# A convolution, a state space layer and a recurrence on one core: decay rates computed behind the first chunk, one zero fill a slot, one staging load for four blocks, a last step in halves

## What is computed

```
# layer 0, added to x: a causal "convolution" over time of cond, per feature, then a state space scan
conv  = conv_b + sum_k x_pad[:, k:k+L, :] * cond[k]        # K = 128 taps
proj  = conv @ Wp + bp ;  B_t = softplus(proj[:64]) ; C_t = tanh(proj[64:])
u     = x @ Ws + bs
A, dt = -softplus(A_log), softplus(dt_log) ; decay = 1 + dt * A      # 64 rates each
state = decay * state + dt * B_t * u_t ;  y_t = C_t * state
x     = x + y @ Wo + bo
# layer 1, added to x: a recurrence over time
h     = tanh(h @ Wh + x_t @ Wx + b)                        # 128 steps, h0 = cond
x     = x + hs
```

## Time and profile before

| | |
|---|---|
| three runs | 1167.56, 1169.76, 1170.22 us; median 1169.76 |
| profiled execution, its own time | 1169.48 us |
| its span in the trace | 1167.7 us |
| mean granted TensorE clock | 0.997 |
| PE busy | 1155.2 us |
| DVE, ACT, POOL busy | 698.9, 579.2, 355.5 us |

### The profile page before, as it was taken

How to read it: one execution, slowest core, us unless ns; L and a number is a source line. 1 busy time by engine, 2 the same in 40 slices (tenths; PEclk the granted TensorE clock), 3 DMA queues, 4 the chain that set the end, 5 groups by cost and what they waited for, 6 DMA issues and landing times.

```text
span 1167.7 us, 16204 instructions
## 1 busy us (share of the span) xinstructions
PE 1155.2 (99%) x6000; PEld 965.6 (83%) x6000; DVE 698.9 (60%) x1110; ACT 579.2 (50%) x856; POOL 355.5 (30%) x202
## 2 busy tenths in 40 slices
PE   8999999999999999999999999999999999999997
PEld 8998999976888888888888888888888888888886
DVE  7767776676555555556565555555555556565553
ACT  6755665574435454544454545435454544454431
POOL 5300005023233333333333333333333333333330
PEclk9999999999999999999999999999999999999999
DMA  8897777612022222222222222222222222222202
GB/s 304 288 328 263 255 262 240 204 35 82 6 97 83 99 77 72 72 72 72 72 72 72 72 72 72 75 97 83 98 77 72 72 72 72 72 72 72 73 36 72
DMA packets 71794, 130.12 MB, mean 111 GB/s; under 512 B 3728, under 2 KB 29328, under 8 KB 71760
## 3 DMA queue, kind: packets, MB, share of 16 engines
q1 hardware_dynamic: 71760, 129.65, 33.4%
HBM read 96.08 MB, written 33.55 MB: 111 GB/s over the span
## 4 chain that ended last, share of the span: by engine, by line
PE 96%; DVE 2%; ACT 1%; DMA 0%; issue 0%; POOL 0%; POOLq 0%; SPq 0%; DVEq 0%
PE bank L904 10%; PE bank L912 10%; PE bank L913 10%; PE bank L898 10%; PE bank L916 10%; PE bank L897 10%; PE bank L813 10%; PE bank L952 5%; PE bank L830 5%; PE bank L873 3%; PE bank L879 3%; PE bank L887 2%; PE bank L888 2%; PE bank L848 2%; PE bank L845 2%; PE bank L846 2%
## 5 line engine op out<-in xcount | busy, mean ns | idle before, releaser
L440 POOL TENSOR_TENSOR x_lo<-x_f,x_hi 128x512 fp32r<-128x512 f32 x128 | 161.8, 1297 | 588.2 <-ACT x_hi L537 588.2
L564 ACT ACTIVATE h_f<-z_f 128x512 f32<-128x512 f32 x128 | 80.9, 632 | 296.7 <-DVE z_f L751 296.7
L912 PE MATMUL bank<-wh_hi,hT_hi 128*128 128x512 f32 x512 | 200.7, 392 | 0.0
L760 DVE TENSOR_TENSOR hT_lo<-bank,hT_hi 128x512 fp32r<-128x512 f32 x128 | 88.5, 691 | 186.8 <-ACT hT_hi L568 186.8
L913 PE MATMUL bank<-wh_lo,hT_hi 128*128 128x512 f32 x512 | 200.0, 391 | 0.0
L898 PE MATMUL bank<-wx_lo,x_hi 128*128 128x512 f32 x512 | 199.7, 390 | 0.0
L897 PE MATMUL bank<-wx_hi,x_hi 128*128 128x512 f32 x512 | 199.6, 390 | 0.0
L751 DVE TENSOR_TENSOR z_f<-bank,b_rows 128x512 f32<-128x512 f32 x128 | 88.5, 691 | 132.3 <-PE bank L916 129.3
L434 POOL TENSOR_TENSOR x_lo<-x_f,x_hi 128x2048 fp32r<-128x2048 f32 x32 | 147.9, 4621 | 1.4 <-PE bank L813 1.4
L904 PE MATMUL bank<-wx_hi,x_lo 128*128 128x512 f32 x512 | 144.8, 404 | 0.3 <-POOL x_lo L440 0.3
L916 PE MATMUL bank<-wh_hi,hT_lo 128*128 128x512 f32 x512 | 137.0, 389 | 0.0
(11 more groups left out here) (93 smaller groups left out, 1682.7 us busy)
## 6 DMA issues: line engine op xcount, KB each, us to landing
x_f<-x_dtb SPq DMA_DIRECT2D x32, 1024.0 KB, 7.9
out<-x_f SPq DMA_DIRECT2D x31, 1024.0 KB, 5.3
ring<-x_rev SPq DMA_DIRECT2D x55, 512.0 KB, 5.2
ring<-hankel SPq DMA_DIRECT2D x44, 512.0 KB, 4.1
x_early<-x_rev SPq DMA_DIRECT2D x8, 512.0 KB, 7.1
t_low<-low_rows SPq DMA_DIRECT2D x4, 512.0 KB, 4.7
wx_f<-Wx SPq DMA_DIRECT2D x1, 1024.0 KB, 8.0
wh_f<-Wh SPq DMA_DIRECT2D x1, 1024.0 KB, 7.8
```

What stands on the lines that cost most here:

```text
L440: nc.gpsimd.tensor_tensor(x1_lo[:, c], x1_f[par][:, c], f(x1_hi[:, c]), ALU.subtract)\
L564: nc.scalar.activation(h_f[:], z_f[:], ACT.Tanh).then_inc(h_ready, 1)
L760: nc.vector.tensor_tensor(hT_lo[:], turned_h, f(hT_hi[:]), ALU.subtract).then_inc(htlo_ready, 1)
L912: nc.tensor.matmul(z, hT_hi[:, k], wh_hi[:, k], start=False, stop=False)
```

## The change

- One load of 512 KB stages the low rows of the first four blocks; it is issued first. The next ones are issued after the `x` of blocks 3, 7, 11 and 15, instead of before the `x` of blocks 2, 6, 10 and 14. `vec` is loaded after block 7's `x` and the third room's low rows, and before the first piece of `Wp`.
- One zero fill a slot, 96 partitions x 768 elements; all four slots before the first shift on DVE.
- The wait for `vec` and the rate instructions move behind chunk 0's copies; ACT's two run after its loop over chunk 1's copies, DVE's last three at the end of chunk 1's projections, ahead of the scaling of `Wo`.
- The last step runs in two halves of 256 columns: bias add, tanh, two transposes, residual add and store, each a half at a time, the two halves' transposes in different banks. `hT_hi` and `hT_lo` of the last step are not computed.

```diff
@@ sync, load_ring
-                if n < 4:
-                    sp.dma_start(low_room(0)[quarter(n)], low_rows[quarter(n)]).then_inc(first_low[n], DMA)
-                if n % 4 == 2 and n // 4 + 1 < SHIFTED // 4:
-                    ...
+                if n == 0:
+                    sp.dma_start(low_room(0), low_rows[0:P]).then_inc(lows_loaded[0], DMA)
                 if n >= SHIFTED:
                     sp.dma_start(t_rows, toeplitz(n)).then_inc(t_loaded[slot], DMA)
                 for half in (range(2) if n == 0 else range(1)):
                     ...
+                if n % 4 == 3 and n // 4 + 1 < SHIFTED // 4:
+                    ...
             for n in range(WIDE):
                 load_ring(n, n % RING)
-                if n == 1:
-                    sp.dma_start(vec[:], vectors).then_inc(vec_loaded, DMA)
+            sp.dma_start(vec[:], vectors).then_inc(vec_loaded, DMA)
@@ sync, last step
+                if last:
+                    rows = out[:, TIME - 1, :].rearrange("(c p) b -> p c b", p=P)
+                    for h in range(2):
+                        sp.wait_ge(out_ready, TIME + h)
+                        sp.dma_start(rows[:, 2 * h:2 * h + 2], x1_f[par][:, 2 * h:2 * h + 2, G - 1]).then_inc(stored[par], DMA)
@@ scalar: the rates
             shift(0)
             shift(1)
-            act.wait_ge(rate_step, 1)
-            ...
-            act.wait_ge(vec_loaded, DMA)
             for m in range(0, BANKS, 2):
                 ...
+            act.wait_ge(vec_loaded, DMA)
             for m in range(BANKS):
                 copy_conv(1, m)
                 copy_turned(0, m)
                 ...
+            act.wait_ge(rate_step, 1)
+            nc.scalar.activation(rates_e[:], rates[:, 0:2], ACT.Exp).then_inc(rate_act, 1)
+            act.wait_ge(rate_act, 1)
+            nc.scalar.activation(rates[:, 2:4], rates_e[:], ACT.Ln, bias=1.0).then_inc(rate_act, 1)
@@ scalar: the last step
+                    if last and s == G - 1:
+                        for h in range(2):
+                            act.wait_ge(zsum_ready, t + 1 + h)
+                            nc.scalar.activation(h_f[:, half_of(h)], z_f[:, half_of(h)], ACT.Tanh).then_inc(h_ready, 1)
+                        continue
@@ vector
             def zero(slot):
-                nc.vector.memset(t_part(slot)[quarter(0), :, 0:3 * Q], 0.0)
-                nc.vector.memset(t_part(slot)[quarter(1), :, 0:2 * Q], 0.0)
-                nc.vector.memset(t_part(slot)[quarter(2), :, 0:Q], 0.0).then_inc(t_zeroed, 1)
+                nc.vector.memset(t_part(slot)[0:3 * Q, :, 0:3 * Q], 0.0).then_inc(t_zeroed, 1)
 ...
-            zero(0)
+            for slot in range(RING):
+                zero(slot)
             shift(0)
-            zero(1)
             shift(1)
-            zero(2)
-            zero(3)
-            dve.wait_ge(vec_loaded, DMA)
-            ...
@@ vector: the last step
+                    if last and s == G - 1:
+                        for h in range(2):
+                            nc.vector.tensor_tensor(z_f[:, half_of(h)], ZB[s % 2][:, half_of(h)], b_rows[:, half_of(h)], ALU.add)\
+                              .then_inc(zsum_ready, 1)
+                        for h in range(2):
+                            dve.wait_ge(ht_done, t + 1 + h)
+                            end = x1_f[par][:, 2 * h:2 * h + 2, s, :]
+                            nc.vector.tensor_tensor(end, last_turned(h).rearrange("p (c b) -> p c b", c=2), end, ALU.add)\
+                              .then_inc(out_ready, 1)
+                        continue
@@ tensor: the last step
+                    if end:
+                        for h in range(2):
+                            pe.wait_ge(h_ready, t + 1 + h)
+                            for k in range(2 * h, 2 * h + 2):
+                                mm = nc.tensor.transpose(HB[1 - h][:, bass.ts(k, P)], h_f[:, bass.ts(k, P)], ident[:])
+                            mm.then_inc(ht_done, 1)
+                        continue
```

More of the change, by code:

```diff
@@ L192, in conv_at, with half_of, last_turned @@
             return conv[:, :, t] if c == 2 else conv[:, t]
+        def half_of(h):
+            return slice(h * D // 2, (h + 1) * D // 2)
+        def last_turned(h):
+            return HB[1 - h][:, half_of(h)]
         def turn_bank(c, m):
@@ L301, in load_ring @@
                 t_rows = ring[:, slot, 0].rearrange("p (j k) -> p j k", j=CH // 2)
-                if n < 4:
-                    sp.dma_start(low_room(0)[quarter(n)], low_rows[quarter(n)]).then_inc(first_low[n], DMA)
-                if n % 4 == 2 and n // 4 + 1 < SHIFTED // 4:
+                if n == 0:
+                    sp.dma_start(low_room(0), low_rows[0:P]).then_inc(lows_loaded[0], DMA)
+                if n >= SHIFTED:
+                    sp.dma_start(t_rows, toeplitz(n)).then_inc(t_loaded[slot], DMA)
+                for half in (range(2) if n == 0 else range(1)):
+                    some = CH // 2 if n == 0 else CH
+                    sp.dma_start(x_part(n)[:, half * some:(half + 1) * some], x_rev[:, bass.ds(n * CH + half * some, some), :])\
+                      .then_inc(x_part_loaded[x_slot(n)] if half == 0 else second_half, DMA)
+                if n % 4 == 3 and n // 4 + 1 < SHIFTED // 4:
                     k = n // 4 + 1
@@ L355, in stores_and_loads @@
                     load_x(g + 2, par)
-                for s in range(0, G, 1 if last else G):
+                for s in range(0, G - 1 if last else G, 1 if last else G):
                     n = 1 if last else G
@@ L381, in shift @@
                     pool.wait_ge(wp_ready, 2)
-                pool.wait_ge(first_low[n] if n < 4 else lows_loaded[n // 4], DMA)
+                pool.wait_ge(lows_loaded[n // 4], DMA)
                 if n >= RING:
@@ L463, in shift @@
                     act.wait_ge(t_zeroed, n + 1)
-                act.wait_ge(first_low[n] if n < 4 else lows_loaded[n // 4], DMA)
+                act.wait_ge(lows_loaded[n // 4], DMA)
                 if n >= RING:
@@ L597, in shift @@
                     dve.wait_ge(t_zeroed, n + 1)
-                dve.wait_ge(first_low[n] if n < 4 else lows_loaded[n // 4], DMA)
+                dve.wait_ge(lows_loaded[n // 4], DMA)
                 if n >= RING:
@@ L646, in _ @@
                 copy_conv(0, m)
+            dve.wait_ge(vec_loaded, DMA)
+            nc.vector.scalar_tensor_tensor(out=rates[:, 0:2], in0=logs, scalar=-1.0, in1=logs, op0=ALU.mult, op1=ALU.min)\
+              .then_inc(rate_step, 1)
             for c in range(KC - 1):
@@ L655, in _ @@
                 if c == 1:
+                    dve.wait_ge(rate_act, 2)
+                    nc.vector.scalar_tensor_tensor(out=rates_e[:], in0=logs, scalar=0.0, in1=rates[:, 2:4], op0=ALU.max, op1=ALU.add)\
+                      .then_inc(rate_step, 1)
+                    dve.wait_ge(rate_step, 2)
+                    nc.vector.tensor_tensor(rates[:, 0:1], rates_e[:, 0:1], rates_e[:, 1:2], ALU.mult).then_inc(rate_step, 1)
+                    dve.wait_ge(rate_step, 3)
+                    nc.vector.tensor_scalar(rates[:, 1:2], rates[:, 0:1], -1.0, 1.0, ALU.mult, ALU.add).then_inc(rate_step, 1)
                     dve.wait_ge(ws_wo_loaded, 2 * DMA)
```

17 lines of the change are left out of this document (1 added, 16 removed).

## The result

The changed kernel takes 1162.91 us (median of 6, 1162.57 to 1163.3) against 1169.97 for the kernel before (6 runs, 1167.56 to 1171.29). (In runs 4 and 8 of the experiments and in the kernel before beside runs 1 to 4, one execution each took over 3000 us; the ratios leave it out, and it moves the medians by 0.12 at most.) The ratio is 0.9941, 95% interval 0.9928 to 0.9954: 6.9 us faster, between 5.4 and 8.4. The forecast was 5.1 us and 1164.4; the time lies 0.3 us inside the lower end of the wide range (1162.6) and under the lower end of the forecast's own (1163.2). The profiled execution took 1162.89 us against 1169.48, 6.6 less, and those are what the two traces share out.

What follows compares the result with a forecast made beforehand. PE, busy 99% of the span, was taken as the bound, with some 12 us winnable at the ends. 1169.48 - 3.15 (start) - 1.95 (end) = 1164.4 us; own range 1163.2 to 1165.4, wide range 1162.6 to 1167.0.

Steps and rivals of the forecast that it cites:

- the pause ahead of block 2: Start: PE idle from 10.63 to 13.54 us behind ACT's late bank copy; the clock's fall loses 1.6 us more.
- The start: Up to block 16: it starts at 37.35 instead of 40.50, held by DMA landings, winning 3.15 us (bounds 0.55 to 4.0).
- the landing rule: First DMAs: a load lands when as many KB were asked for before and with it, whatever they are.
- rival B: Behind block 4: DMA engines take the front's gain back, leaving 1.45 us; time 1166.1, or 1167.0 at 318 GB/s; chance 0.15.
- the new wait ahead of block 4: Low rows land at 13.65, ACT's shift and copy take 1.65, so PE starts block 4 at 15.35 instead of 18.75.
- Block 0: Start: the staging load lands at 4.4, so PE starts block 0 at about 6.4, 1.3 us later than before.
- The rates' new place: Chunks 1 and 2: late rate instructions cost nothing, ACT being idle and DVE having 0.85 us of cover for 0.54.
- The end: Last step: halves and dropping `hT_hi` and `hT_lo` win 1.95 us, bounds 1.3 and 2.4.
- S: Slower: low rows of blocks 4 to 7 land after 19.2; with block 4 at 22, 1172 us; chance 0.03.
- C: Start: PE's idle time ahead of block 0 delays the clock one stretch, costing about 1 us; 1165.5; chance 0.10.
- D: End: halves don't do what they say, winning 1.0 to 1.3 instead of 1.95; 1165.2; chance 0.07.
- F: Faster still: landings 0.9 us sooner without vec's 13-element rows, and a last landing of 1.6; 1163; chance 0.05.

Runs made afterwards that it cites:

- run 4: Changed kernel with three zero fills a slot instead of one, all four slots still ahead of DVE's first shift; 1166.87 us, ratio 0.9978.
- run 8: Kernel before with only the single staging load and the new order of the low rows; 1170.35 us, ratio 1.0003.
- run 1: Changed kernel with the last step whole again, as before the change; 1164.51 us, ratio 0.9958.
- run 2: Changed kernel with the rates computed ahead of chunk 0 again and vec loaded after block 1's x; 1163.17 us, ratio 0.9947.
- run 3: Changed kernel with the low rows in four 128 KB quarter loads and the old load order again; 1165.53 us, ratio 0.9974.
- run 9: Kernel before with only the rates and vec moved behind chunk 0; 1167.93 us, ratio 0.9987.
- run 10: Changed kernel plus an unneeded 256 KB load to partitions 0 to 63, behind block 1's x; 1164.45 us, ratio 0.9961.
- run 11: Changed kernel plus an unneeded 256 KB load to partitions 32 to 95, behind block 1's x; 1162.64 us (two executions), ratio 0.9943.
- run 6: Changed kernel with the staging load in two: partitions 0 to 63 first, 64 to 127 behind block 1's x; 1164.45 us, ratio 0.9953.
- run 12: Changed kernel with first low rows as 256 KB to partitions 32 to 95, then two 128 KB loads behind block 1's x; 1164.34 us, ratio 0.9954.
- run 5: Changed kernel with the first low rows in four 128 KB quarter loads, all issued first; 1164.31 us, ratio 0.9951.
- run 7: Changed kernel with 10 warming matmuls instead of 8; 1163.14 us, ratio 0.9943.

## Why the prediction was right in kind and short in size

**What bounds the kernel, and the pause ahead of block 2: right, with one correction.** The rates' chain held block 2. Run 8 has it with fast loads, run 9 takes it away and the x load is late next. But run 2 shows that the chain was long because of DVE's twelve fills between the shifts, not for the wait on `vec`: in run 8 DVE's last fill ends at 11.1 and the first rate instruction follows at once, in run 2 it waits for `vec` and starts at 7.72; moving the rates and shortening the fills are two cures of one illness.

**The start: 4.71 us instead of 3.15; the step that failed is the landing rule.** I took it that "a load lands when as many KB have been asked for before it and with it, whatever they are", and that from block 4 on the engines move 358 GB/s. The second was what PE asked for: run 4, whose loads had come at 418 GB/s, drops to 352 from 20 us on, when its late PE sets the pace. The first was wrong in its last three words. In the old queue stood loads to a quarter of the partitions. Runs 10 and 11, alike but for the partitions (and the rows that the extra load reads), show that a load to one side of partition 64 slows what is queued with it. Runs 3, 6, 9 and 12 and the trace of the kernel before agree, 234 to 331 GB/s in 6.5 to 9.9 or 9.9 to 13.3 us, where the runs without such loads have 355 to 420; run 5 agrees in the rate, 277, but not in the time. Each of these figures is from one execution. The Trainium skill (SBUF — State Buffer, Door 1: The DMA port swizzle) says this: partitions 0 to 63 are behind 8 of 16 DMA ports, no more than 0 to 31, and 64 to 127 behind the other 8. Runs 10 and 11 agree with it: partitions 0 to 63 lie behind one group of ports, 32 to 95 behind both, and the rates are 192 and 387 GB/s. The Trainium skill speaks there of the bandwidth of such loads themselves; what the runs add is that full loads around them are slowed too. The figure of the Trainium skill (DMA: Bandwidth & Descriptors, Specifications) by which I weighed rival B, about 358 GB/s, was no limit here: 415 GB/s stood for 15 us.

With the faster landings my own steps give the measured start, so what was missing was the landings' 1.6 us and not a further wait. The low rows of blocks 4 to 7 were at 12.1 instead of 13.65, ACT's three copies end at 13.7, and PE reached block 4 only at 14.04: the new wait ahead of block 4, which I had as the end of the chain, was not one. The chain went through x of block 1 (8.38) and three and more blocks of PE. Block 16, which I had waiting for the DMA engines, waited for nothing.

**Block 0: near.** 5.77 against 6.4, the staging load at 4.15 against 4.4, the x of block 1 at 8.4 against 9.1, fills done at 4.1 against 4.2. The fill on 96 partitions takes what it takes on 32: 3.12 for four with their gaps.

**The rates' new place: right.** Nothing is lost there. ACT's activations lie in its idle time, and DVE's remainder has 0.4 us left of 0.85.

**The end: right.** 2.07 against 1.95. A half costs DVE 0.38 and ACT 0.37 instead of 0.42, the last residual add ends 2.16 us after the first bias add (2.3 predicted), and 128 KB land in 1.8 (1.95).

**The sum.** The start was 1.56 us short, the end 0.12, and 0.18 went the other way: 1.50, which is what lies between 1164.4 and the profiled 1162.89. The range held the time by 0.3 us; its lower end was not worked out from what happened, so that it held is in part luck. Three slips in the working changed nothing: it is four blocks and not twelve that ask for 2.62 MB each 7.25 us, the issue of one of the four small loads took SP 0.74 us and not under 0.5, and by its own terms S's case of block 4 at 22 is 1169.48 + 3.25 - 1.95 = 1170.8, not 1172.

**The rivals.** B did not come, and by run 3 not even the slow loads starve PE for long behind block 4: 0.21 us ahead of block 10. C, the late clock, is real as a mechanism (runs 2, 4 and 6, and a fall in run 5) but not in the changed kernel's own trace. In run 2 it came with 0.95 us of idle time ahead of block 0, made block 4 1.3 us later in that trace, and did not show in the median. D and S did not come. F, "faster still", is where the time fell, but not for its reason: run 2 clears `vec`. Its 0.05 was too little; I had no price for what the quarter loads did to their neighbours, though the landing of the second one, 4.6 us where the first took 2.3, stood there to be asked about.

## What to carry to other kernels

Look at GB/s beside the DMA share: a share of 1 at 320 GB/s is not a full queue but a slow one, and a small load to partitions 0 to 63, or to fewer of them, can be what slows the large ones around it. Stage such data for several uses in one load over all partitions, even if it comes a microsecond later for the first. Two causes in a row (slow loads, and an instruction chain ahead of the first copy) hide each other: in the medians the loads alone gave 0 and the rates alone 1.2 us, while all parts of the start together brought block 16 forward by 4.7. (In one trace each, the two alone brought it forward by 1.6 and 1.7.) When the chain at the end of a kernel is one tile handed from engine to engine, halves and leaving out what nobody reads were worth 2 of 6.7 us together; no run has one without the other.

## What the runs showed of the hardware

- The same 256 KB load to 64 partitions cost the queue half its rate at partitions 0 to 63 (192 GB/s from 6.5 to 9.9 us) and nothing at 32 to 95 (387), and a load issued ahead of it landed 2.0 us later than with the other (1.4 later than in the changed kernel).
- 412 to 420 GB/s into one core from 9.9 to 35 us, but 254 from 4.5 to 6.5 us of the same trace, with loads queued.
- DVE's fill of 768 elements: 0.7 us on 32 partitions as on 96.
- The first record of TensorE's clock lay at 4.6 us in the changed kernel and at 5.8, 9.9, 14.6, 10.0 and 7.4 in runs 1, 2, 4, 6 and 7; until it, the granted column reads 1.00 while PE works at half its pace (17 or 18 records in 3.40 us instead of 32, runs 2, 4 and 6). PE had stood idle ahead of block 0 for 0.75, 0.46, 0.95, 3.54, 0.67 and hardly any time in them: the longest pause has the latest record, but the rest are not in order.
